# Context products six slots and strip results seven slots behind a tile's scores, in place of five and six

## The reference

```
x = x + x_n * gate            # x_n = group_norm(x); gate = sigmoid of a small deformable
                              # 1-d convolution over the 128 channel means, one gate per channel
y = group_norm(x)
value = conv1x1(y)                          # 64 channels
key, query = relu(bn(conv1x1(relu(bn(conv1x1(y))))))     # 64 channels each
# 27 neighbours of each pixel: 3x3 with dilation 1, 2 and 4, zero padded
sim = softmax over the 27 of <key[neighbour], query>
context = sum over the 27 of sim * value[neighbour]
x = x + conv1x1(context)                    # back to 128 channels
```

## Time and profile before

| | us |
|---|---|
| median of 3 runs | 1745.24 (1743.99 to 1748.65) |
| the profiled execution, its own time | 1741.07 |
| its span, first to last instruction | 1739.3 |
| PE busy | 1619.8, 93% |
| VectorE busy | 1236.3, 71% |
| ScalarE busy | 1172.1, 67% |
| GpSimd busy | 793.0, 46% |
| DMA queue q1, share of 16 engines | 38.4% |

### The profile page before, as it was taken

One profiled execution on the slowest core, in us unless ns is written; L12 is line 12 of the kernel. 1 busy time (PEld: TensorE's weight loads), 2 busy tenths in 40 slices (PEclk: granted clock), 3 DMA queues, 4 the chain that ended last, 5 costly groups with the idle time before them and its releaser, 6 DMA issues.

```text
span 1739.3 us, 36776 instructions
## 1 busy us (share of the span) xinstructions
PE 1619.8 (93%) x10439; PEld 1337.4 (77%) x10439; DVE 1236.3 (71%) x4518; ACT 1172.1 (67%) x3044; POOL 793.0 (46%) x1759
## 2 busy tenths in 40 slices
PE   1799999999999999999999999999999999999998
PEld 1587877787777878777878777878777878777876
DVE  5477777777777777777777777777777777777665
ACT  2566666766666766676766676766676766676775
POOL 4545454345454445454444454444454444454430
PEclk9999999999999999999999999999999999999999
DMA  3234442434443434443434443434443433433223
GB/s 117 47 94 130 124 136 86 139 89 131 128 131 89 139 87 131 132 127 94 138 88 127 133 121 103 135 90 127 133 117 106 124 101 122 139 99 124 84 68 116
DMA packets 73557, 197.67 MB, mean 114 GB/s; under 512 B 11536, under 2 KB 52880, under 8 KB 65168
## 3 DMA queue, kind: packets, MB, share of 16 engines
q1 hardware_dynamic: 73360, 195.32, 38.4%
HBM read 51.62 MB, written 51.38 MB: 59 GB/s over the span
## 4 chain that ended last, share of the span: by engine, by line
PE 66%; issue 9%; POOL 9%; DVE 7%; ACT 7%; DMA 1%; SPq 0%; ACTq 0%; DVEq 0%; POOLq 0%
PE ps_o L417 17%; PE ps_s L384 15%; PE ps_v L451 10%; PE ps_p L434 7%; PE ps_p L429 7%; PE ps_t L396 6%; POOL hats L704 4%; DVE e L905 2%; ACT eT L564 2%; POOL hats L703 2%; ACT hats L610 2%; ACT e L549 1%; ACT qq L575 1%; ACT kk L586 1%; PE ps_v L477 1%
## 5 line engine op out<-in xcount | busy, mean ns | idle before, releaser
L549 ACT ACTIVATE e<-e,zmin 128x256 f32<-128x256 f32 x800 | 406.2, 508 | 448.0 <-DVE zmin L905 442.5
L417 PEld LDWEIGHTS ps_o<-eT,v 128*128 128x128 f32 x3584 | 478.0, 192 | 110.9 <-issue 58.3
L417 PE MATMUL ps_o<-eT,v 128*128 128x128 f32 (+1 forms) x3584 | 528.8, 275 | 22.2 <-ACT eT L564 18.4
L905 DVE CUSTOM_DVE_ANT_0 e<-ps_s,mask 128x256 f32<-128x256 f32 x800 | 336.0, 420 | 283.0 <-PE ps_s L384 276.2
L384 PE MATMUL ps_s<-kk,qq 128*128 128x256 f32 x1408 | 438.7, 393 | 2.1 <-DVE zmin L905 2.1
L918 DVE TENSOR_SCALAR e<-e,rz 128x256 f32<-128x256 f32 x800 | 340.0, 425 | 0.0
L451 PE MATMUL ps_v<-wvox,xb 128*128 128x128 f32 x2048 | 274.6, 277 | 47.8 <-DVE r_row L996 46.2
L396 PE MATMUL ps_t<-ident,e 128*128 128x128 f32 x1600 | 305.8, 273 | 0.0
L451 PEld LDWEIGHTS ps_v<-wvox,xb 128*128 128x128 f32 x2048 | 252.8, 193 | 68.6 <-issue 66.9
L396 PEld LDWEIGHTS ps_t<-ident,e 128*128 128x128 f32 x1600 | 225.7, 141 | 80.8 <-issue 0.6
L384 PEld LDWEIGHTS ps_s<-kk,qq 128*128 128x128 f32 x1408 | 221.6, 192 | 38.1 <-issue 35.3
(11 more groups left out here) (154 smaller groups left out, 1638.8 us busy)
## 6 DMA issues: line engine op xcount, KB each, us to landing
raw<-in_x_dram SPq DMA_DIRECT2D x32, 1568.0 KB, 8.7
out_dram<-raw SPq DMA_DIRECT2D x32, 1568.0 KB, 5.4
v<-v SPq DMA_DIRECT2D x192, 256.0 KB, 3.7
kk<-kk SPq DMA_DIRECT2D x192, 112.0 KB, 2.2
ksp<-kk SPq DMA_DIRECT2D x192, 64.0 KB, 2.6
kk<-kk SPq DMA_DIRECT2D x32, 224.0 KB, 3.0
w_s<-in_w_dram SPq DMA_DIRECT2D x1, 64.0 KB, 6.4
wv_s<-in_wv_dram SPq DMA_DIRECT2D x1, 64.0 KB, 5.3
```

The costliest lines, as they stand in the source:

```text
L417: last = nc.tensor.matmul(o[:, UPIX * max(0, c - 1):UPIX * min(UNITS, c + 1)], v[:, s, c, :], eT[:, UPIX * (base + a):UPIX * (base + b)], ...
L549: nc.scalar.activation(e[:, i, :], e[:, i, :], ACT.Exp, bias=zmin[:, i:i + 1], scale=-1.0, accum_out=zs[:, i:i + 1]).then_inc(e_done.next( ...
L905: nc.vector.tensor_tensor_reduce(e[:, i, :], ps_s[(TILES * n.parity() + t) % 2][:, 0:KEYS], mask[:].rearrange("p s h a b -> p (s h a b)"), ...
```

## The change

Two constants. SCALE and TRANSPOSE stay. No instruction is added or removed; `context` on PE moves one slot later, and with FINAL so do `final` on DVE and the store on SP. The tail after the last image grows from 7 to 8 slots.

```
-SCALE, TRANSPOSE, CONTEXT, FINAL = 1, 3, 5, 6
+SCALE, TRANSPOSE, CONTEXT, FINAL = 1, 3, 6, 7
```

## The result

The changed kernel takes 1867.2 us (median of 4, 1862.1 to 1873.8) against 1744.6 for the kernel before: a ratio of 1.070, 95% interval 1.066 to 1.074, 7% slower. 1878 had been predicted, with a range of 1815 to 1920. A later run of the same file gave 1873.0 and 1.072 (1.069 to 1.075).

What follows compares the result with a forecast made beforehand. PE was taken to set the pace, busy 93% of the span, so the change could act only through its waits. Terms -2 + 18 + 18 + 61 + 38 = +133 us gave 1878 us, range 1815 to 1920.

Steps and rivals of the forecast that it cites:

- The wait that goes: PE's wait for the eT copy, mostly slot 2: removing it gains 0 in steady state, -2 us in all.
- Slot 24: Strip 4's final enters DVE's gapless stretch behind L974, delaying PE 0.60 us in 30 images: +18 us.
- Slots 17 to 18: Strip 2's final lands ahead of values of block 0 on DVE, delaying PE about 0.60 us an image: +18 us.
- The sign that went with it: Slots 17 to 18: values (L451) would wait for DVE's v, 0.6 us, 31 times.
- The store: SP, slot 6: store 2.8 us later, ahead of key copies; scores of tile 10 1.98 us later an image: +61 us.
- The clock: Slot 10: longer idle time drops PE's clock to 1.2 GHz in 25 images, 1.5 us each: +38 us.
- The line of the clock in the 40 slices: Sign: in the profile's 40 slices, a PE clock under full in many.
- The sum: All terms together: -2 + 18 + 18 + 61 + 38 = +133 us, giving 1878 us.
- Rival (a): Slot 10: clock stays up because two shorter idle stretches are not one long one; 1840 us, chance 0.26.
- (d), faster: Slot 2: the eT wait was real and hid not late behind it, copies hidden; 1725 us, chance 0.04.

Runs made afterwards that it cites:

- finals-only run: Kernel before with only FINAL raised to 7 (finals and store later), CONTEXT staying 5; 1855.4 us, ratio 1.064.
- filler kernel: Changed kernel plus three TensorE products ahead of the scores of tile 10 in each image, inside the wait for key copies; 1827.0 us, again 1824.8.
- context-only run: Kernel before with only CONTEXT raised to 6, FINAL staying 6; 1725.5 us, ratio 0.988.
- kernel with the copies first: Changed kernel with SyncE's store put behind the key and value copies of its slot; 1748.3 us, ratio 1.001.

## Why the prediction was right, and where its terms were off

The direction, the cause and nearly the size were right: 133 us forecast, 123 measured. That the total is so near is in part luck, since errors of its terms cancelled. Step by step:

- **The wait that goes: wrong.** The step said "Gain 0" in the steady state and -2 in all. The context's move alone is worth 21 us. The reading of slot 2 holds (L434 waits for hid there), but I took the 34 idle places of PE for all that wait for eT and did not look at the weight loads, which wait in 101. About 13 us of the gain are the period's; some of the rest, not separated, belongs to slot 10.
- **Slot 24: right.** +18 us; 0.61 us an image measured by taking the collision away. In the finals-only run the same 18 us stand in the wait for eT, 36.2 us where it was 18.4.
- **Slots 17 to 18: right in kind, mis-sized.** +18 forecast, 8 measured. Two parts of it were off. The scaling ahead of `final` takes 0.56 us in about 20 of the images and 0.35 in most others where I had kept 0.79, and PE starts 0.05 us behind the end of DVE's addition (894.37 and 894.42 in the rows below), where I had assumed r_row's 0.26 and so no slack. The sign that went with it, a wait of L451 for DVE's v 31 times, did not come in the rows of products (1.4 us, once).

```profile
892.62 0.56 DVE L918 TENSOR_SCALAR e<-e,rz 128x256 f32<-128x256 f32 x1
893.10 0.67 DVE L924 SCALAR_TENSOR_TENSOR raw<-raw,g,ps_o 128x448 f32<-128x448 f32 x1
893.69 0.68 DVE L937 TENSOR_TENSOR v<-ps_v,bias 128x512 f32<-128x512 f32 x1
```
```profile
894.42 1.16 PE L451 MATMUL ps_v<-wvox,xb 128*128 128x128 f32 x8
```

- **The store: right, its mechanism and its size.** 2.8 us later on SP, the second copy landing 6.4 to 8.4 us behind the store's issue, on average 6.8 and 7.0 in the two traces where it was 7.13, so that the nearer issue of the copies brought it 0.3 us at most. 1.98 us an image forecast; 1.85 in the first trace of the changed kernel and 1.98 in the second, 55 and 59 us for the 30 images behind a store (61 forecast). In all of them PE starts 0.04 us behind the landing. The wait for r_row is still 1.3 to 1.5 us behind it.
- **The clock: right in kind, too small.** 38 us forecast; 48 measured against the filler kernel, and about 6 more for the four falls that kernel still has. The falls were 27, I had said 25; but I had priced each by the one of before, 1.7 us of missing clock, and in 18 of the 27 the clock stayed down for twice as long: (0.34 + 0.50 + 0.50 + 0.37) x 2 = 3.4 us in the windows above. It falls during the wait for r_row, just behind its end or earlier, and the products behind it are done at 1.2 GHz. (The wait in front of the fall of before was 0.20 us by the start of the scores, with 0.04 of it idle time of the products, not the 0.25 that I had read.) The line of the clock in the 40 slices, which I had named as a sign, reads 9 throughout, before and after, and tells nothing; the mean, 0.997 and 0.957, does.
- **The sum.** -21 + 18 + 8 + 57 + 54 = 116, against 123 by the medians; 7 us stand in no term. From run to run the steps are -21 (the context), +23 (the finals), +76 (the wait and four falls) and +48 (the other falls), 126. Of the forecast's terms that for eT was 19 too high, slot 17's 10 and the store's 4, the clock's 16 too low: half of the error cancelled.

Rival (a), that the clock stays up, was the filler kernel's case: it gives 1825 to 1827, with four falls left; 1840 had been worked out. (d), faster, fell; but its half on the eT wait was right, and the context's move alone would have made the kernel faster.

## What to carry to other kernels

A lag that moves one computation also moves the DMA tied to it, and on an in-order issue queue what counts is which slot's other issues it lands in front of: look up, for each copy behind it, how long before its reader it lands. Where a large store is put ahead of small copies that somebody waits for soon, put it behind them; here that alone was worth 120 us. Look first at who waits for the store: here it is the load of the image four later, into the same buffer, and SP's rows show no wait of it. For waits of TensorE read the rows of weight loads too, since a short wait there can leave no idle time in the rows of the products.

## What the runs showed of the hardware

- The first small copy (kk, 112 KB, 2.2 us to landing at the median) issued behind a 1568 KB store lands 5.8 us behind the store's issue (mean of 31, 5.79 in both), whether it is issued 0.76 us behind it, as before, or 0.45, as in the changed kernel. The store itself mostly lands after 5.4 us; in 7 of the 31 images of before it lands later than this copy (5.8 to 6.4). The issue of a ksp copy takes 1.4 us on SP behind the store, and 0.6 mostly otherwise. The Trainium skill, "DMA: Bandwidth & Descriptors", section "Queues, rings and completion order", has descriptors consumed in ring order on each DMA engine, and completion not in the order of issue over the engines; the landings fit both.
- A fall of the clock has a price of its own, here almost as large as the wait that brings it: 48 against 60 us. It came in 27 of the 30 images of the changed kernel in which 1.3 to 3.1 us idle, 0.65 of work and 1.3 to 1.5 idle followed each other; in 15 of 31 in the finals-only run, with mostly 1.1 to 1.2 us in front; in 4 where three products were put into the first wait; in 1 image each of the kernel before and of the context-only run, whose scores start 0.2 and 0.6 us late; and in none where 1.49 us stood alone, as in the kernel with the copies first.
